# Latent attention on one core: which query tiles share a column tile in the value products

## The reference

```
ql  = x @ Wqd;  q  = ql @ Wqu (16 heads of 16);  qr = rope(ql @ Wqr) (16 heads of 64)
ckv = x @ Wkvd; k  = ckv @ Wku; v = ckv @ Wvu (16 heads of 16);  kr = rope(x @ Wkr) (shared)
scores = (q.k + qr.kr) * scale, causal: a query sees only keys up to its own position
out = softmax(scores) @ v, heads side by side, then @ Wo, added to x
```

## Time and profile before

| what | value |
|---|---|
| median of 3 runs | 1435.81 us (1435.34 to 1439.43) |
| profiled execution, span | 1435.6 us; no other time of it is recorded, and the median lies 0.2 us above |
| PE busy | 1349.0 us, 94% of the span |
| DVE, ACT, POOL busy | 895.4, 694.1, 278.4 us |
| mean granted clock of TensorE | 0.984 of full speed |
| latent attention heads | about 1045 us to 1274 us of the span |

### The profile page before, as it was taken

The page is one execution under the profiler, slowest core; times in us unless marked ns, Lnnn a source line. Parts: engine busy times, 40 slices in busy tenths (PEclk is TensorE's granted clock), DMA queues, the critical chain, the costliest instruction groups (busy, mean ns, idle before and its releaser), DMA issues. The chain is left out here.

```text
span 1435.6 us, 32894 instructions
## 1 busy us (share of the span) xinstructions
PE 1349.0 (94%) x13699; PEld 738.4 (51%) x13707; DVE 895.4 (62%) x2147; ACT 694.1 (48%) x1037; POOL 278.4 (19%) x343
## 2 busy tenths in 40 slices
PE   7999998999679988999999989999899999989999
PEld 3355555474345774563555554436355555555436
DVE  3899994666486456749999826433655555535431
ACT  5487776646483325535777752111444444442110
POOL 4322513001230000043000000110533433210110
PEclk9999999999879999999999999999999999999999
DMA  3323300100300000022222030000300000000000
GB/s 87 70 38 65 65 14 1 34 1 2 118 0 4 17 1 16 0 45 42 43 39 36 3 117 0 1 0 7 64 13 17 15 13 14 9 1 1 1 0 29
DMA packets 33957, 37.47 MB, mean 26 GB/s; under 512 B 9153, under 2 KB 24626, under 8 KB 33810
## 3 DMA queue, kind: packets, MB, share of 16 engines
q1 hardware_dynamic: 33810, 35.39, 11.2%
HBM read 18.43 MB, written 1.07 MB: 14 GB/s over the span
## 5 line engine op out<-in xcount | busy, mean ns | idle before, releaser
L616 DVE TENSOR_REDUCE row_max_pieces<-psum 128x1 f32<-128x512 f32 (+3 forms) x672 | 406.9, 647 | 112.4 <-PE psum L510 109.7
L717 ACT ACTIVATE probs<-psum 128x1024 f32<-128x1024 f32 (+7 forms) x384 | 343.7, 900 | 212.6 <-PE psum L510 212.2
L564 PE MATMUL psum<-probs,v_ones 128*32 128x256 f32 (+1 forms) x2688 | 238.8, 376 | 9.0 <-POOL probs L499 4.6
L510 PE MATMUL psum<-q_all,k_head 97*32 97x512 f32 (+3 forms) x1536 | 190.7, 487 | 0.0
L510 PE MATMUL psum<-k_stack,q_stack 96*32 96x512 bf16 x2048 | 158.8, 379 | 3.5 <-DMA k_stack<-arena 1.3
L510 PE MATMUL psum<-q_stack,k_stack 97*32 97x512 bf16 x2048 | 157.8, 379 | 0.0
L564 PEld LDWEIGHTS psum<-probs,v_ones 128*32 128x32 f32 x2688 | 88.0, 109 | 85.1 <-POOL probs L499 21.6
L510 PE MATMUL psum<-k_head_bf,q_all_bf 80*32 80x512 bf16 (+3 forms) x768 | 93.0, 328 | 2.3 <-ACT k_head_bf L2487 1.1
L510 PEld LDWEIGHTS psum<-q_all,k_head 97*32 97x32 f32 x1536 | 78.8, 109 | 29.5 <-issue 3.9
L510 PEld LDWEIGHTS psum<-k_stack,q_stack 96*32 96x32 bf16 x2048 | 56.5, 95 | 72.1 <-DVE row_max_pieces L616 20.4
L510 PEld LDWEIGHTS psum<-q_stack,k_stack 97*32 97x32 bf16 x2048 | 58.3, 96 | 49.4 <-ACT probs L717 3.7
(11 more groups left out here) (368 smaller groups left out, 2085.6 us busy)
## 6 DMA issues: line engine op xcount, KB each, us to landing
q_stack<-arena SPq DMA_DIRECT2D x32, 96.0 KB, 2.7
k_stack<-arena SPq DMA_DIRECT2D x32, 96.0 KB, 2.6
arena<-gd_g_sums SPq DMA_DIRECT2D x6, 512.0 KB, 6.1
q_stack<-arena SPq DMA_DIRECT2D x32, 64.0 KB, 2.3
k_stack<-arena SPq DMA_DIRECT2D x32, 64.0 KB, 2.3
x_tokens<-in_x SPq DMA_DIRECT2D x4, 256.0 KB, 3.6
k_stack<-arena SPq DMA_DIRECT2D x32, 32.0 KB, 2.3
q_stack<-arena SPq DMA_DIRECT2D x32, 32.0 KB, 2.0
```

The costliest lines, as they stand in the source:

```text
L510: last = pe.matmul(o[j:j + 32], by[:, j:j + 32], rows, **flags)
L564: last = pe.matmul(psum[32 * g:32 * g + VW, PVB, a - g * D:D], V[:, c, h, :], pr[:, n % PB, a:(g + 1) * D], start=(c == 0), stop=(c == (2 ...
L616: last = dve.reduce_max(mx[:, h % 2, qt, i:i + 1], o[:, 0:plain], AX.X)
L717: act.activation(pr[:, n % PB, q_from(c):], psum[:, 2 * (n % 2):2 * (n % 2) + 2, :].rearrange("p a n -> p (a n)")[:, q_from(c):], ACT.Exp, ...
```

## The change

Column tile g holds query tiles g and g + 4 in the causal layer. `values_of(c, g)` gives the blocks that chunk c touches: both where c <= g, the second alone where g < c <= g + 4, none beyond. The two blocks of a matmul are then 512 columns apart in `probs`, and side by side in PSUM as before. The place in O follows (`tile_of`). The other two attention layers keep their assignment (`"(g b)"`, `(0, 2)`).

```diff
@@ attention_heads
+    tile_of = "(b g)" if causal else "(g b)"
+    by_group = lambda a: a.rearrange(f"p ({tile_of[1:-1]} n) -> p g b n", b=2, n=P)
+
+    def values_of(c, g):
+        return (sum(4 * b + g < c for b in range(2)), 2) if causal else (0, 2)
+
@@ values(n)
-                    for g in range(q_from(c) // D, 4):
-                        a = max(q_from(c), g * D)
-                        last = pe.matmul(psum[32 * g:32 * g + VW, PVB, a - g * D:D], V[:, c, h, :],
-                                         pr[:, n % PB, a:(g + 1) * D], start=(c == 0),
-                                         stop=(c == (2 * g + 1 if causal else NT - 1)))
+                    for g in range(4):
+                        first, end = values_of(c, g)
+                        if first < end:
+                            last = pe.matmul(psum[32 * g:32 * g + VW, PVB, first * P:end * P].rearrange(
+                                                 "p (b n) -> p b n", n=P), V[:, c, h, :],
+                                             by_group(pr[:, n % PB, :])[:, g, first:end], start=(c == 0),
+                                             stop=(c == (g + 4 if causal else NT - 1)))
                     last.then_inc(pv_ready, 1)
@@ turned(h)
-                                O[:].rearrange("p (g b) n -> p b g n", b=2)[:, b, :, (h - 2) * HD:(h - 1) * HD],
+                                O[:].rearrange(f"p {tile_of} n -> p b g n", b=2)[:, b, :, (h - 2) * HD:(h - 1) * HD],
```

## The result

In 20 runs each, the median went from 1437.47 us to 1430.3 us. The ratio of the changed kernel to the one before is 0.995, with a 95% interval from 0.9936 to 0.9964: faster by 0.4 to 0.6%. Forecast were 1429.1 us and 0.47% less. The medians lie 7.2 us apart, where 6.7 was forecast.

What follows compares the result with a forecast made beforehand. PE was taken to set the pace in the latent stage. Savings of 14 x 0.42 + 0.59 + 0.21 = 6.7 us bring the span from 1435.6 to 1428.9, median 1429.1 us; range 1425.3 to 1432.4.

Steps and rivals of the forecast that it cites:

- The 0.64 a head: Value products of chunks 4 to 6 on tile 3: shorter passes save 0.213 us a chunk, 10.2 us for 16 heads.
- Added loads: 192 more weight loads on tiles 0 to 2: hidden under short passes, cost nothing; rival that they don't hide, 1435.8, chance 0.06.
- split operand: Value products reading two blocks 512 columns apart: cost nothing; rival that tile 3 pays 20.5 us more, 1449.6 us, chance 0.04.
- V(4)'s: Value product of chunk 4: its 0.21 us becomes a wait for DVE on PE, but moves K(7) 0.21 earlier.
- D: Piece of row maxima after K(7): its load waits for DVE to free the ring, so it stays at 1174.52.
- K(7): Key scores of chunk 7, after V(4): come 0.21 us earlier and start POOL's chain, on which V(6) hangs.
- V(6): Value product of chunk 6: waits 0.35 us for POOL with rotary work, starts 0.21 earlier; its own 0.21 is kept.
- V(5)'s: Value product of chunk 5, behind D: PE arrives 0.21 us earlier at V(6), which waits for POOL; kept without rotary work.
- head 15: Last head: the value product of chunk 7 waits for the last zeroing, which hangs on K(7); saves 0.21 us.
- head 14: Head without row maxima left and no D: 0.38 of 0.42 remains, V(6) adds 0.21, together 0.59 us.
- all of it counts: Rival: the waits at D and for POOL are looser than shown, so 10.2 us is saved; 1425.6 us, chance 0.15.
- one more wait takes over: Rival: V(6)'s saving is lost to POOL at chunk 7's value product; 1431.6 us, or 1432.5 in all heads; chance 0.18.

Runs made afterwards that it cites:

- the third assignment: Changed kernel, but column tile g holds query tiles g and 7 - g: 14.87 us a head with rotary work, 13.15 without; ratio to the kernel before 0.9941.
- the three lengthened chunks: Changed kernel with V(4), V(5) or V(6) long again on tile 3: 15.09, 14.88, 15.09 us a head with rotary work; 13.15, 13.37, 13.37 without.
- the run with blocks side by side: Changed kernel, two-block products reading 256 adjacent columns: 14.88 us a head with rotary work and 13.15 without, against 14.87 and 13.16.
- taking the waits away: Changed kernel with POOL's rotary additions one chunk later, or V(5) ahead of the row maxima: 14.35 or 14.89 us a head with rotary work; ratios 0.9905, 0.9954.
- POOL later, old assignment: Kernel before the change with POOL's rotary additions one chunk later: 14.77 us a head with rotary work, 13.58 without; ratio 0.995.
- both edits: Changed kernel, POOL's rotary additions one chunk later and V(5) ahead of the row maxima: 14.15 us a head with rotary work, 12.96 without; ratio 0.9894.

## Why the prediction was right

- *What bounds.* PE sets the pace, and the fullest column tile sets PE's. Shown by the change itself, and by the third assignment from the other side.
- *The 0.64 a head.* 0.21 or 0.22 a chunk, shown by each of the three lengthened chunks in the heads where it counts.
- *Added loads and split operand: nothing.* Shown by the passes 0.11 apart and by the run with blocks side by side. (Line 1497, from which the second was read, has other shapes, 32 rows and 128 weight columns; the run decides it.) The rule of the Trainium skill on loads ("TensorE: Matmul & The Clock Gate", Part 3, "What overlaps and what doesn't"), overlap only where the row group differs, does not hold for column tiles in this kernel: loads of 109 ns run beside passes that start 0.11 us apart, on the same rows.
- *Which wait takes which saving.* PE loses V(4)'s at D, but K(7) carries it through POOL to V(6) in heads with rotary work; there V(5)'s is lost at POOL; V(6)'s is kept. Shown chunk by chunk, in both kinds of head, and again by taking the waits away. 14.88 was forecast for a head with rotary work and 14.87 measured; 0.42 less in heads without, and 0.42 measured (13.58 to 13.16).
- *The sum.* 6.7 us forecast, 6.7 in the profiled stage; 0.47% forecast, 0.5% in the ratio. That the tenths agree is in part luck. The twelve heads with rotary work gave 5.11 where 12 x 0.42 = 5.04 was forecast, heads 12 and 13 gave 0.84 as forecast, and head 15 gave 0.22 for 0.21. But head 14 gave 0.51 (from its turn to the transposes of head 15: 1256.27 to 1267.90 before, 1252.36 to 1263.47 after) for 0.59; where the 0.08 went is open.
- *The term that was mis-sized.* "PE stood idle 0.35 us before 1177.69, so PE's own arrival was at 1177.34": it was 1177.18. It did no harm, since V(6) hung on POOL by either number, but it made the wait look a third smaller than it is, and with it what an edit on POOL is worth: 0.53 a head from the fourth on, 0.65, 0.52 and 0.82 in the first three (15.20, 15.28 and 15.59 fall to 14.55, 14.76 and 14.77), and 6.8 us in the stage. That is as much as the change under study. (Rows 5 give 0.39 for passes merged from three tiles; the 0.38 of one pass is in rows 7.)

The rivals "all of it counts" and "one more wait takes over" fall with the measured turns. The first of them, though, is what the kernel turns into when both waits are removed: a head then goes from 14.77 (POOL later, old assignment) to 14.15, which is 0.62 of the 0.64. The two differ in the place of V(5) as well, and the old assignment with both edits was not run, so a hundredth or more of the 0.62 may be that edit's.

## What to carry to other kernels

When matmuls on column tiles run side by side, count the columns of the fullest tile chunk by chunk: spreading a triangle so that neighbours share no tile shortens it, levelling the totals doesn't. Then follow the saving through one period to the next instruction that waits for another engine; a saving ahead of such a wait is worth nothing unless something on the waited-for chain also moves. And in one in-order queue, put long optional work behind the short item that the bounding engine needs next: moving POOL's additions by one place was worth as much here as the change to the matmuls (6.8 and 6.7 us in the stage).

## What the runs showed that was not expected

An idle time before a matmul, as the profile gives it, is shorter than the time lost, by the fixed part of a matmul (0.16 us here, 0.35 shown against 0.53 gained by removing it). And the periods of this long loop are far steadier than the run: turn to turn repeats to 0.02 us once the first three heads are over, while the start of the stage lay between 1042.3 and 1047.7 us in executions whose programs have the same instructions of the same sizes up to there.
